# A four-layer LoRA kernel on one core: x laid out batch by batch on chip, six of its tiles issued from the sync queue, one weight split moved to GpSimd

## The reference

```python
x = x + einsum('bsi,boi->bso', x, L0_weight[ids0])       # layer 0: a full 512x512 matrix for every batch
x = x + x @ W1.T + 2.0 * gated_lora(x, Wr, A, B)          # layer 1: 8 experts of rank 16, two of them gated per token
x = x + x @ W2.T + bias + 0.5 * (x @ A2[ids2]) @ B2.T     # layer 2: rank 32
x = x + down(silu(gate(x)) * up(x))                       # layer 3: 1376 wide; gate, up, down each with a rank-16 adapter
```

## Time and profile before

| | us |
|---|---|
| median of 3 runs (lowest, highest) | 321.08 (320.62, 321.49) |
| the profiled execution | 321.29 |
| its span, first to last instruction | 319.5 |
| TensorE busy in the span | 310.6 |
| VectorE busy | 151.4 |
| ScalarE busy | 107.4 |
| GpSimd busy | 15.4 |
| mean granted clock of TensorE (1 is 2.4 GHz) | 0.989 |

### The profile page before, as it was taken

One profiled execution on the slowest core, in us unless ns is written; L12 is line 12 of the kernel. 1 busy time (PEld: TensorE's weight loads), 2 busy tenths in 40 slices (PEclk: granted clock), 3 DMA queues, 4 the chain that ended last, 5 costly groups with the idle time before them and its releaser, 6 DMA issues.

```text
span 319.5 us, 4612 instructions
## 1 busy us (share of the span) xinstructions
PE 310.6 (97%) x1672; PEld 257.0 (80%) x1672; DVE 151.4 (47%) x251; ACT 107.4 (34%) x165; POOL 15.4 (5%) x23
## 2 busy tenths in 40 slices
PE   5898999999999999999999999999999999999996
PEld 4366788888888888888888888888889788897886
DVE  0088897885769446364254254254624531011101
ACT  0277662513446247144144144145325220000000
POOL 2542000200100000000000000000000000000000
PEclk9599999999999999999999999999999999999999
DMA  5999982005203500422421421550642001000111
GB/s 132 364 330 312 373 266 71 0 0 171 94 0 101 157 10 0 130 78 58 131 78 54 131 84 47 148 163 0 173 140 90 2 0 66 35 33 2 55 44 35
DMA packets 24016, 33.21 MB, mean 104 GB/s; under 512 B 3264, under 2 KB 16320, under 8 KB 23872
## 3 DMA queue, kind: packets, MB, share of 16 engines
q1 hardware_dynamic: 19776, 30.90, 30.4%
q10 hardware_dynamic: 4224, 2.10, 2.3%
HBM read 30.89 MB, written 2.10 MB: 103 GB/s over the span
## 4 chain that ended last, share of the span: by engine, by line
PE 95%; DMA 2%; DVE 1%; SPq 1%; issue 0%
PE bank L945 24%; PE bank L946 24%; PE bank L947 24%; PE bank L1090 3%; PE bank L1046 3%; PE bank L899 3%; PE bank L992 2%; DMA w_raw<-in_w 2%; PE bank L921 2%; PE bank L918 2%; PE bank L929 2%; PE bank L931 1%; PE bank L930 1%; PE bank L879 1%; SPq L297 1%; PE bank L1113 1%
## 5 line engine op out<-in xcount | busy, mean ns | idle before, releaser
L945 PE MATMUL bank<-xb,wgu_hl 128*128 128x512 f32 x176 | 69.1, 392 | 0.0
L946 PE MATMUL bank<-xb,wgu_hl 128*128 128x512 f32 x176 | 69.0, 392 | 0.0
L947 PE MATMUL bank<-xb,wgu_hl 128*128 128x512 f32 x176 | 68.5, 389 | 0.0
L947 PEld LDWEIGHTS bank<-xb,wgu_hl 128*128 128x128 f32 x176 | 33.1, 188 | 7.2
L804 DVE TENSOR_TENSOR act_f<-bank,act_f 128x512 f32<-128x512 f32 x22 | 15.2, 691 | 48.2 <-PE bank L1046 46.4
L945 PEld LDWEIGHTS bank<-xb,wgu_hl 128*128 128x128 f32 x176 | 33.0, 188 | 5.8
L946 PEld LDWEIGHTS bank<-xb,wgu_hl 128*128 128x128 f32 x176 | 33.2, 189 | 5.3
L945 PE MATMUL bank<-act_hl,wd_hl 128*128 128x512 f32 (+1 forms) x99 | 36.6, 370 | 0.0
L946 PE MATMUL bank<-act_hl,wd_hl 128*128 128x512 f32 (+1 forms) x99 | 36.2, 366 | 0.0
L947 PE MATMUL bank<-act_hl,wd_hl 128*128 128x512 f32 (+1 forms) x99 | 36.2, 366 | 0.0
L406 ACT ACTIVATE act_hl<-act_f 128x512 f32 (+1 forms) x22 | 13.9, 632 | 61.7 <-DVE act_f L804 61.7
(11 more groups left out here) (127 smaller groups left out, 449.5 us busy)
## 6 DMA issues: line engine op xcount, KB each, us to landing
w_raw<-in_w SPq DMA_DIRECT2D x22, 256.0 KB, 7.0
wgu_raw<-in_wgu SPq DMA_DIRECT2D x11, 512.0 KB, 3.5
bgu_raw<-in_bgu SPq DMA_DIRECT2D x88, 64.0 KB, 2.2
w_raw<-in_w SPq DMA_DIRECT2D x7, 512.0 KB, 6.3
x_f<-in_xT ACTq DMA_DIRECT2D x8, 256.0 KB, 8.4
out<-x_f SPq DMA_DIRECT2D x7, 256.0 KB, 2.1
wd_own<-in_wd SPq DMA_DIRECT2D x2, 704.0 KB, 4.8
wd_raw<-in_wd SPq DMA_DIRECT2D x2, 704.0 KB, 4.4
```

The costliest lines, as they stand in the source:

```text
L945: pe.matmul(dst, w_hi, x[0][:, cols], start=start, stop=False)
L946: pe.matmul(dst, w_hi, x[1][:, cols], start=False, stop=False)
L947: return pe.matmul(dst, w_lo, x[0][:, cols], start=False, stop=stop)
```

## The change

`x_f` becomes `[B, C, S]`: the four chunks of one batch lie together, so that an x tile is one run of 2 KB in each partition where it was four runs of 512 B. ScalarE's queue issues the x tiles 0 and 1 only; tile b from 2 on is issued by the sync queue, ahead of the waits for weight b's place in the ring and ahead of weight b. The split of aw1 leaves ScalarE and VectorE and becomes two GpSimd instructions after its split of x tile 2, behind a wait for aw1's transfer, with a semaphore of its own (`aw1_split`), on which TensorE waits ahead of the first `thin1`. Everywhere else the same elements are addressed in the new layout: in layers 1 to 3 the additions into `x_f` and the splits of it walk through four runs of 128 elements 2 KB apart, and so do the stores of the result, which take 512 B runs from the chip's memory.

```diff
--- before.py
+++ after.py
@@ -81,7 +81,7 @@
         o_misc = o_ad + 11 * KB
 
 
-        x_f = at("x_f", o_xf, [C, T])
+        x_f = at("x_f", o_xf, [B, C, S])
         xa = at("xa", o_xa, [2, C, T], F32R)
         xb = at("xb", o_xb, [2, C, T], F32R)
 
@@ -187,7 +187,7 @@
         const_step, ident_ready, masks_ready, iota_ready = (sem(n) for n in (
             "const_step", "ident_ready", "masks_ready", "iota_ready"))
         t3_zeroed, td_zeroed = sem("t3_zeroed"), sem("td_zeroed")
-        x0_hi, x0_lo = sem("x0_hi"), sem("x0_lo")
+        x0_hi, x0_lo, aw1_split = sem("x0_hi"), sem("x0_lo"), sem("aw1_split")
 
         w0_raw_used, l0_tm, l0_tr = sem("w0_raw_used"), sem("l0_tm"), sem("l0_tr")
         l1_tm, l1_tr = sem("l1_tm"), sem("l1_tr")
@@ -228,13 +228,20 @@
             return bank[4 + j if h == 0 else j]
 
 
-        splits = ["aw1"] + [f"w1_{o}" for o in range(C)] + ["b1", "a2"] + [f"w2_{o}" for o in range(C)] + ["b2", "agu"]
+        def by_batch(tokens):
+
+            return tokens.rearrange("p (b s) -> p b s", s=S)
+
+        def x_f_tokens(o, cols):
+
+            return x_f[:, cols.start // S:cols.stop // S, o]
+
+
+        splits = [f"w1_{o}" for o in range(C)] + ["b1", "a2"] + [f"w2_{o}" for o in range(C)] + ["b2", "agu"]
         nth = {name: i + 1 for i, name in enumerate(splits)}
 
         def split_views(name):
 
-            if name == "aw1":
-                return aw1_raw[:], aw1_hl[:, :, 0], aw1_hl[:, :, 1]
             if name == "b1":
                 return b1_raw[:], b1_hl[:, 0], b1_hl[:, 1]
             if name == "a2":
@@ -247,7 +254,7 @@
             o = int(name[3:])
             return raw[:, o], hl[:, 0, o], hl[:, 1, o]
 
-        split_source = {"aw1": (aw1_in, 16), "b1": (b1_in, 16), "a2": (a2_in, 16 * B), "agu": (agu_in, 16 * B),
+        split_source = {"b1": (b1_in, 16), "a2": (a2_in, 16 * B), "agu": (agu_in, 16 * B),
                         "b2": (b2_in, 16)}
         for o in range(C):
             split_source[f"w1_{o}"] = (w1_in[o], 16)
@@ -306,6 +313,8 @@
                 sp.dma_start(w0_raw[0][:, c], w0[adapter0[0]][:, c * D:(c + 1) * D]).then_inc(w0c_in[c], 16)
             for b in range(1, B):
                 adapter = adapter0[b]
+                if b >= 2:
+                    sp.dma_start(x_f[:, b], xT[b]).then_inc(x_in[b], 16)
                 if b == W0_RING:
                     sp.wait_ge(l0_tm, 1)
                 if b > W0_RING:
@@ -372,7 +381,7 @@
             sp.dma_start(wd_raw[3][:], wd[3]).then_inc(wd_in[3], 16)
             for i, (o, cols) in enumerate(DOWN_PIECES):
                 sp.wait_ge(x3_sum, i + 1)
-                sp.dma_start(out[o, :, cols], x_f[:, o, cols]).then_inc(out_sent, 16)
+                sp.dma_start(out[o, :, cols].rearrange("p (b s) -> p b s", s=S), x_f_tokens(o, cols)).then_inc(out_sent, 16)
             sp.wait_ge(out_sent, 16 * len(DOWN_PIECES))
 
 
@@ -387,10 +396,16 @@
             for b in range(1, B):
                 cols = slice(b * S, (b + 1) * S)
                 pool.wait_ge(x_in[b], 16)
-                pool.tensor_copy(xa[:, 0, 1:C, cols], x_f[:, 1:C, cols]).then_inc(x0_hi, 1)
+                pool.tensor_copy(xa[:, 0, 1:C, cols], x_f[:, b, 1:C]).then_inc(x0_hi, 1)
                 pool.wait_ge(x0_hi, b)
-                pool.tensor_tensor(xa[:, 1, 1:C, cols], x_f[:, 1:C, cols],
+                pool.tensor_tensor(xa[:, 1, 1:C, cols], x_f[:, b, 1:C],
                                    xa[:, 0, 1:C, cols].bitcast(F32), ALU.subtract).then_inc(x0_lo, 1)
+                if b == 2:
+                    pool.wait_ge(aw1_in, 16)
+                    pool.tensor_copy(aw1_hl[:, :, 0], aw1_raw[:]).then_inc(aw1_split, 1)
+                    pool.wait_ge(aw1_split, 1)
+                    pool.tensor_tensor(aw1_hl[:, :, 1], aw1_raw[:], aw1_hl[:, :, 0].bitcast(F32),
+                                       ALU.subtract).then_inc(aw1_split, 1)
             pool.wait_ge(l0_tr, B)
             pool.wait_ge(w12_lo, nth["a2"])
             pool.memset(t3_st[:].bitcast(F32), 0.0).then_inc(t3_zeroed, 1)
@@ -420,17 +435,15 @@
             def x1_high(b):
                 cols = slice(b * S, (b + 1) * S)
                 act.wait_ge(x1_sum, b + 1)
-                high(xb[:, 0, :, cols], x_f[:, :, cols]).then_inc(x1_hi, 1)
-
-
-            for b in range(B):
-                act.dma_start(x_f[:, :, b * S:(b + 1) * S], xT[b]).then_inc(x_in[b], 16)
+                high(xb[:, 0, :, cols], x_f[:, b]).then_inc(x1_hi, 1)
+
+
+            for b in range(2):
+                act.dma_start(x_f[:, b], xT[b]).then_inc(x_in[b], 16)
 
             for b in range(1, B):
                 if b > W0_RING:
                     act.wait_ge(l0_tm, b - W0_RING + 1)
-                if b == 3:
-                    split_hi("aw1")
                 for k in range(KC):
                     if k == KC - 1:
                         copy_y0(b - 1)
@@ -457,9 +470,10 @@
 
             def x_high(l, h, o):
                 n = number(l, h, o)
-                dst = (xa if l == 1 else xb)[:, 0, o, h * HT:(h + 1) * HT]
+                cols = slice(h * HT, (h + 1) * HT)
+                dst = (xa if l == 1 else xb)[:, 0, o, cols]
                 act.wait_ge(x_sum, n + 1)
-                high(dst, x_f[:, o, h * HT:(h + 1) * HT]).then_inc(x_hi, 1)
+                high(by_batch(dst), x_f_tokens(o, cols)).then_inc(x_hi, 1)
 
 
             router_exp(0)
@@ -600,15 +614,14 @@
                     low(lo, raw, hi).then_inc(w12_lo, 1)
 
             def x1_add(b):
-                cols = slice(b * S, (b + 1) * S)
                 dve.wait_ge(l0_tr, b + 1)
-                dve.tensor_tensor(x_f[:, :, cols], bank[2 + b % 2][:].rearrange("p (c t) -> p c t", c=C),
-                                  x_f[:, :, cols], ALU.add).then_inc(x1_sum, 1)
+                dve.tensor_tensor(x_f[:, b], bank[2 + b % 2][:].rearrange("p (c t) -> p c t", c=C),
+                                  x_f[:, b], ALU.add).then_inc(x1_sum, 1)
 
             def x1_low(b):
                 cols = slice(b * S, (b + 1) * S)
                 dve.wait_ge(x1_hi, b + 1)
-                low(xb[:, 1, :, cols], x_f[:, :, cols], xb[:, 0, :, cols]).then_inc(x1_lo, 1)
+                low(xb[:, 1, :, cols], x_f[:, b], xb[:, 0, :, cols]).then_inc(x1_lo, 1)
 
             def sum_ranks1(h, j):
 
@@ -639,8 +652,6 @@
             last.then_inc(masks_ready, 1)
 
             for b in range(1, B):
-                if b == 3:
-                    split_lo("aw1")
                 for k in range(KC):
                     dve.wait_ge(w0_hi, KC * (b - 1) + k + 1)
                     low(w0_hl[b % W0_RING][:, 1, k], w0_raw[b % W0_RING][:, 1 + k],
@@ -701,12 +712,12 @@
 
             def x_add(l, h, o):
                 n = number(l, h, o)
-                dst = x_f[:, o, h * HT:(h + 1) * HT]
+                dst = x_f_tokens(o, slice(h * HT, (h + 1) * HT))
                 dve.wait_ge(main_done, n + 1)
                 if l == 1:
-                    ins = dve.tensor_tensor(dst, bank[4 + n % 4][:], dst, ALU.add)
+                    ins = dve.tensor_tensor(dst, by_batch(bank[4 + n % 4][:]), dst, ALU.add)
                 else:
-                    ins = dve.scalar_tensor_tensor(out=dst, in0=bank[4 + n % 4][:], scalar=bias_sb[:, o:o + 1],
+                    ins = dve.scalar_tensor_tensor(out=dst, in0=by_batch(bank[4 + n % 4][:]), scalar=bias_sb[:, o:o + 1],
                                                    in1=dst, op0=ALU.add, op1=ALU.add)
                 ins.then_inc(x_sum, 1)
 
@@ -714,7 +725,7 @@
                 cols = slice(h * HT, (h + 1) * HT)
                 xs = xa if l == 1 else xb
                 dve.wait_ge(x_hi, number(l, h, o) + 1)
-                low(xs[:, 1, o, cols], x_f[:, o, cols], xs[:, 0, o, cols]).then_inc(x_lo, 1)
+                low(by_batch(xs[:, 1, o, cols]), x_f_tokens(o, cols), by_batch(xs[:, 0, o, cols])).then_inc(x_lo, 1)
 
 
             router(0)
@@ -830,9 +841,9 @@
 
             def x3_add(i):
                 o, cols = DOWN_PIECES[i]
-                dst = x_f[:, o, cols]
+                dst = x_f_tokens(o, cols)
                 dve.wait_ge(down_done, i + 1)
-                dve.tensor_tensor(dst, down_bank(o, cols), dst, ALU.add).then_inc(x3_sum, 1)
+                dve.tensor_tensor(dst, by_batch(down_bank(o, cols)), dst, ALU.add).then_inc(x3_sum, 1)
 
             t3_uv_low(0)
             t3_low(0)
@@ -915,10 +926,10 @@
                 if b == 0:
                     for c in range(C):
                         pe.wait_ge(w0c_in[c], 16)
-                        ins = pe.matmul(bank[0][:], x_f[:, c, cols], raw[:, c], start=(c == 0), stop=(c == C - 1))
+                        ins = pe.matmul(bank[0][:], x_f[:, b, c], raw[:, c], start=(c == 0), stop=(c == C - 1))
                 else:
                     pe.wait_ge(w0_in[b % W0_RING][0], w0_landed(b))
-                    pe.matmul(bank[b % 2][:], x_f[:, 0, cols], raw[:, 0], start=True,
```

(3 more changed lines are left out.)

## The result

The changed kernel takes 319.57 us (median of 8 runs, 318.82 to 320.28); the kernel before took 320.99 (8 runs, 320.53 to 321.49). The ratio is 0.9953, 95% interval 0.9938 to 0.9967: faster by 1.4 us. The forecast was 6.0 faster, so its sign was right and its size wrong. The profiled execution took 319.52 with a span of 317.7, again 1.8 outside it, and 1.8 less than the profiled one before.

A forecast was written before the change was run, and what follows sets the result against it. TensorE's own work was taken to bound the kernel from 28 us on, so only earlier time could be won: 321.29 - 6.4 (batch 3's product earlier) + 0.1 (last store) = 315.0 us, range 313.0 to 319.0.

The forecast's parts named there:

- Queue order, the rate: Start of layer 0: transfers behind the first chunk run at 390 GB/s, so weight 0's last chunk lands at 8.5 us.
- chunk 0: First of weight 0's four transfers: with only two x tiles ahead, it lands at 6.5 us instead of 9.05.
- the 11.2 of the sum: Batch 1's weight is completely landed at 11.2 us, 2.7 us after weight 0's last chunk.
- The first chunk stays late: Rival, chance 0.13: weight 0's own first packets are slow, it lands at 9.0 and the clock falls; 2.1 earlier, 319.3 us.
- The clock: TensorE in batch 0: full clock, since it stands still for only 0.8 us instead of 3.3; batch 0 ends at 9.4.
- Sync queue, costed at nothing: Six more transfers issued there, about 3 us over 20, cost nothing because the backlog of transfers hides them.
- The moved split: aw1's pair on GpSimd takes 2.1 us, delays x tile 3's split and costs about 1 us at batch 3.
- From there the old order of work follows at its old pace: Behind batch 3's product, ending at 21.8 us, 6.4 earlier than before, the work continues at its old pace.
- the layout at nothing: Additions into `x_f` for 512 columns take 0.69 us either way, so the new strides cost nothing.
- the end: The last store, cut into 512 B runs instead of 1 KB, costs between nothing and 0.3 us; 0.1 taken.
- no hole of TensorE past 28 us: From 28 us on TensorE's own work fills the time; a new wait there would make the forecast wrong.
- no half clock all through: Against the slower rival, chance 0.03: TensorE at half clock throughout batches 0 to 3, 5.7 us later, 327 us.

The follow-up runs named there:

- layout_only: The changed kernel with aw1's split put back and all eight x tiles on ScalarE's queue, so only the layout differs from before; 320.82 us, 0.9994.
- whole0: The changed kernel with weight 0 fetched by one 1 MB transfer in 8 KB runs instead of four chunks; 321.83 us, 1.0015 against the kernel before.
- order_only: The kernel before with the queue order alone: x tiles 2 to 7 on the sync queue, still 512 B runs; 319.48 us, 0.9968.
- fix_no_warm: The changed kernel with aw1's split put back, weight 0 as one transfer, late id loads and 9 warm-up matmuls; 318.95 us, 0.9941.
- ids_late_after: The changed kernel with the ids of layers 2 and 3 read behind layer 1's weight transfers; 319.33 us, 0.9940 against the kernel before.
- aw_back: The changed kernel with aw1's split given back to ScalarE and VectorE; 319.92 us, 0.9972 against the kernel before.
- aw3_ids: The changed kernel with late id loads and GpSimd's aw1 pair moved behind its split of x tile 3; 320.0 us, 0.9967.
- fix_all: The changed kernel with aw1's split put back, late id loads, weight 0 as one transfer and 18 warm-up matmuls; 317.61 us, 0.9895.
- ids_late_order: The kernel before with the queue order alone and the ids of layers 2 and 3 read behind layer 1's weights; 318.74 us, 0.9935.
- ido_warm14: The kernel before with the queue order alone, late id loads and 14 warm-up matmuls instead of 9; 318.97 us, 0.9935.
- hold1: The changed kernel with the sync queue waiting for all of weight 0 before it issues more; 323.5 us, 1.0082 against the kernel before.
- before_fixed: The kernel before with weight 0 as one transfer, 18 warm-up matmuls and late id loads; 321.99 us, 1.0027.

## Why the prediction was wrong in size

- **Queue order, the rate: the step that failed.** "I take 390" for the transfers behind chunk 0, from slices past 10 us. From 4 to 11 us it was 221, and chunk 3 came at 12.0 instead of 8.5. Of these 3.5 us the rate explains 1.4 (15 engines were done at 9.9); the other 2.1 are one DMA engine, and that the engines might not end together was put at nothing. The row that was nearest in time stood in the forecast: 292 GB/s in the slice from 3 us, and 126 and 148 in the two after it, which I put down to sharing alone. The sharing with x delayed chunk 0, which came at 6.55 as forecast (`layout_only` puts it back to 9.97); it did not explain the slow rate. With one transfer of 8 KB runs the window moves 315 and weight 1 follows by 11.5, near the 11.2 of the sum. The rival "The first chunk stays late" had slow first transfers as its cause, with the wrong chunk. That its 319.3 is nearest to the result is luck: its chunk 0 at 9.0 and its clock that falls did not happen in the change.
- **The clock: assumed, and wrong too, but hidden.** "batch 0 ends at 8.5 + 0.88 = 9.4 at full clock". Batch 0 began at half clock, in the change until 9.9 us and in `whole0` until 14.0; in others the clock rose about the warm-up's end and fell again, while TensorE waited (at 8.0 us in `layout_only`) or up to 1.6 us after (`order_only`, `fix_no_warm`, `ids_late_after`), and in `aw_back` and `aw3_ids` it stayed full. I had read a stop of 3.3 us ahead of the half clock as its only cause, and had not asked how late the warm-up raises it: its 18 short passes took 4.21 us, where `fix_all`'s next 18 took 2.17. In the change it costs little, for chunk 3 is later than the passes anyway; with the whole transfer and the late ids it is 1.3 us.
- **Sync queue, costed at nothing.** I counted the issues and missed the register loads on the same queue. In the change they leave the hole from 19.5 us, but moving them gave only 0.4 us, since batch 3 is late already; with the other edits in place they cost 0.9, and `whole0`'s loss of 2 us is gone in `fix_no_warm`, where they are late.
- **The moved split: right in mechanism, its net price not as forecast.** The pair took 2.4 us for the 2.1 of the sum, x tile 3's split waited behind it, and batch 3 took 5.34 us against 5.1. But taking it back gains nothing: VectorE, with the aw1 part on it, is as late at the next batches (`aw_back` waits for it 2.5 us).
- **"From there the old order of work follows at its old pace": not quite.** x tiles that arrive just ahead of use put GpSimd's splits beside VectorE's subtractions up to 46 us. That took 0.2 of the 2.06 us.
- **Right:** chunk 0; the layout at nothing (`layout_only` 0.9994; the additions into `x_f` still 0.69 us); the end, 2.87 us behind the last matmul's start before and 2.98 after (0.1 in the sum); no hole of TensorE past 28 us; no half clock all through.

Still open is why the first transfers are so slow: run length and the number of transfers changed together in `whole0`. The chunks alone are not enough as an answer, for `order_only`, `ids_late_order` and `ido_warm14` have the same four chunks with 512 B x tiles on the same queue and moved 275, 258 and 283 GB/s. Open too is why one DMA engine finishes chunk 3 2.1 us behind the others in the change; in `aw_back` and `aw3_ids`, with the same chunks and x layout, the last two are 0.06 and 0.16 us apart there. The longer warm-up paid only together with the whole transfer and the late ids. The last 2.6 us between `fix_all` and the forecast are placed by the profile (batch 0's late start, then VectorE), but no run takes them back all at once.

## What to carry to other kernels

A rate read from a full pipeline is no rate for the first microseconds: for a chain that starts there, take the rows nearest in time, and test one large transfer against several chunks. When an order is pulled forward, walk each queue that it crosses instruction by instruction, register loads included, and ask of each engine whether it has slack at the new pace. If several obstacles stand one behind another, each mended alone can show next to nothing: mend all of them, then take back one at a time, each of them.

## What had not been expected of the hardware

- Four chunks of 256 KB in 2 KB runs at the start moved 221 GB/s from 4 to 11 us, and 194 to 243 in the five other kernels with the same chunks and x layout (174 in `hold1`, which idles); one transfer of 1 MB in 8 KB runs gave 309 to 316 in six kernels with the new order and landed at 8.1 to 8.3 us.
- A transfer is as late as its last engine: 15 of 16 had ended chunk 3 at 9.9 us, one at 12.03, and one engine ended later than the others on each transfer up to weight 3 (20.53 against 21.96 us). In the six kernels with the 1 MB transfer and the new order the last two engines were at most 0.11 us apart up to aw1's landing; in `before_fixed` 1.4 us on weight 0.
- With the new queue order chunk 0 landed at 7.3 to 7.7 us behind x tiles 0 and 1 in 512 B runs (three kernels), at 6.5 to 6.9 behind 2 KB runs (seven).
- 18 warm-up passes over 4.2 us did not always bring the full clock: it was recorded between 4.5 and 6.4 us in some profiles, and only at 9.9, 10.0, 10.9, 11.2 and 14.0 in five others. Where it came early it could fall again (at 8.8 us in `fix_no_warm`, where TensorE had waited 2.7 us until 8.3; at 13.2 in `ids_late_after`, 1.6 us after a wait of 1.73).
- Four register loads of ids on the sync queue held it for 4.6 us under load, 0.83 to 1.65 us each; in `whole0` 5.6 us, the longest 2.85.
- GpSimd's copy of 128x384 took 0.96 us beside VectorE's subtractions instead of 0.50, and VectorE's three subtractions 2.7 to 3.8 us instead of 2.1.
